# Attention followed by a feed-forward layer: the first feed-forward tile prepared inside the last attention pairs

## The reference

```
xn  = layernorm(x)                                  # eps 1e-5
q   = xn @ q_w.T + q_b
xd  = depthwise conv of xn over tokens, width 3, stride 2   # 1024 keys
k,v = xd @ k_w.T + k_b,  xd @ v_w.T + v_b
att = softmax(q k^T / 8)  v        # 16 heads of 64
A   = att @ out_w.T + out_b
e   = argmax(xn @ W_router)        # one of 4 experts per token
h   = gelu(xn @ W1[e] + b1[e])     # 1024 -> 4096
F   = layernorm(h @ Wo + bo + xn)  # 4096 -> 1024, eps 1e-12, gamma, beta
out = x + A + F
```

## Time and profile before

| | |
|---|---|
| median of 3 runs | 1966.93 us |
| lowest, highest | 1964.63, 2223.03 us |
| the profiled execution's own time | 1971.07 us |
| its span, slowest core (core 3) | 1969.5 us |
| spans of the eight cores | 1947.0 to 1969.5 us |
| busy on core 3: TensorE, VectorE, ScalarE, GpSimd | 93%, 47%, 45%, 15% |

### The profile page before, as it was taken

How to read it: one execution, slowest core, us unless ns; L and a number is a source line. 1 busy time by engine, 2 the same in 40 slices (tenths; PEclk the granted TensorE clock), 3 DMA queues, 4 the chain that set the end, 5 groups by cost and what they waited for, 6 DMA issues and landing times.

```text
span 1969.5 us, 37041 instructions; the slowest of 8 cores (1947.0 to 1969.5 us)
## 1 busy us (share of the span) xinstructions
PE 1828.8 (93%) x12540; PEld 1004.3 (51%) x12540; DVE 934.0 (47%) x1257; ACT 895.2 (45%) x1381; POOL 298.3 (15%) x357
## 2 busy tenths in 40 slices
PE   3588999998999999887899999999999999999995
PEld 1245222232554222222566666766666676666663
DVE  3354689856563888774132233413333323332225
ACT  2244988887455977775122222322222322222221
POOL 3122001001230110011001111101111111101111
PEclk9799999999999999998999999999999999999998
DMA  7759989984686999954756566856555776556551
GB/s 172 182 150 122 181 159 172 162 156 144 183 174 138 141 167 169 166 184 156 260 195 216 203 213 215 266 207 218 211 204 186 249 263 212 183 188 208 203 197 72
DMA packets 89171, 366.69 MB, mean 186 GB/s; under 512 B 11792, under 2 KB 11936, under 8 KB 68000
## 3 DMA queue, kind: packets, MB, share of 16 engines
q1 hardware_dynamic: 50112, 252.06, 38.8%
q0 software_dynamic: 38880, 112.27, 29.7%
HBM read 363.27 MB, written 94.90 MB: 233 GB/s over the span
## 4 chain that ended last, share of the span: by engine, by line
PE 73%; DMA 10%; DVE 6%; ACT 6%; issue 3%; POOL 0%; SPq 0%; DVEq 0%; ACTq 0%; POOLq 0%
PE ff_py L981 25%; PE ff_pu L946 25%; ACT pbuf L556 5%; DMA xa_d<-stg 4%; PE ps_a L505 4%; PE ps_s L543 4%; PE ps_a L569 4%; PE ps_q L367 3%; DMA row<-x 3%; DVE rc L581 3%; PE ps_q L395 2%; PE ps_m L574 2%; PE ps_q L381 2%; DMA xn_d<-row 2%; DMA stg<-x 1%
## 5 line engine op out<-in xcount | busy, mean ns | idle before, releaser
L960 ACT ACTIVATE ff_it<-ff_pu,b1t 128x256 bf16<-128x256 f32 (+1 forms) x608 | 244.3, 453 | 729.6 <-PE ff_pu L946 729.6
L556 ACT ACTIVATE pbuf<-ps_s 128x1024 bf16<-128x1024 f32 x512 | 477.3, 1061 | 116.8 <-PE ps_s L543 99.4
L946 PE MATMUL ff_pu<-ff_xg,ff_w 128*128 128x256 bf16 (+1 forms) x4864 | 516.4, 265 | 1.1 <-DVE ff_xg L930 1.1
L981 PE MATMUL ff_py<-ff_wo,ff_it 128*128 128x512 bf16 x2240 | 510.7, 381 | 3.8 <-DVE stg L511 3.8
L946 PEld LDWEIGHTS ff_pu<-ff_xg,ff_w 128*128 128x128 bf16 x4864 | 444.9, 98 | 73.4 <-issue 1.3
L981 PEld LDWEIGHTS ff_py<-ff_wo,ff_it 128*128 128x128 bf16 x2240 | 218.7, 98 | 238.2 <-issue 8.1
L581 DVE RECIPROCAL rc<-ps_m 128x512 f32<-128x512 f32 x64 | 214.7, 3355 | 44.9 <-PE ps_m L574 44.2
L569 PE MATMUL ps_a<-pbuf,v_sb 128*64 128x512 bf16 x1024 | 209.1, 404 | 5.8 <-DVE masks_all L464 4.8
L543 PE MATMUL ps_s<-qT,kT 64*128 64x512 bf16 x1024 | 201.3, 384 | 11.9 <-ACT pbuf L556 9.7
L574 PE MATMUL ps_m<-pbuf,ones 128*64 128x512 bf16 x1024 | 197.7, 381 | 0.0
L930 DVE COPY ff_xg<-ff_pt 128x1024 bf16<-128x1024 bf16 x35 | 24.2, 691 | 348.0 <-PE ff_pt L923 348.0
(11 more groups left out here) (135 smaller groups left out, 1238.7 us busy)
## 6 DMA issues: line engine op xcount, KB each, us to landing
ff_w<-scrW SPq DMA_DIRECT2D x152, 1024.0 KB
scrW<-w POOLq DMA_DIRECT2D x64, 512.0 KB, 15.6
row<-x SPq DMA_DIRECT2D x32, 512.0 KB, 6.6
xn_d<-row SPq DMA_DIRECT2D x32, 512.0 KB, 5.8
row<-xn_d SPq DMA_DIRECT2D x32, 512.0 KB, 15.8
stg<-x SPq DMA_DIRECT2D x32, 512.0 KB, 12.1
xa_d<-stg SPq DMA_DIRECT2D x32, 512.0 KB, 8.9
scrWo<-wo POOLq DMA_DIRECT2D x16, 512.0 KB, 13.0
```

The costliest lines, as they stand in the source:

```text
L556: e_at[g] = op("scalar", lambda s: s.activation(pbuf[g % 4][:, :], ps_s[g % 2][:, :], AF.Exp, scale=0.125), w)
L946: E.emit("tensor", lambda t, r_=r, q_=q, ic_=ic, c=cc, j_=j, sl=k % NW1SLOT: t.matmul(pu[r_][:, q_, 0:n], w1[:, sl, c * 512 + ic_ * 128:c ...
L960: E.emit("scalar", lambda s, r_=r, q_=q, ic_=ic, i_=i, j_=j, k_=k: s.activation(it[:, k_ % 3, ic_, 0:n], pu[r_][:, q_, 0:n], AF.Gelu, bias ...
L981: E.emit("tensor", lambda t, a_=a, o=oh, ic_=ic, i_=i, k_=k: t.matmul(py[:, 2 * a_ + o, :], it[:, k_ % 3, ic_, a_ * 128:(a_ + 1) * 128], w ...
```

## The change

Three things. The first tile's halves are cast in chunk 3 and transposed in chunk 6 of the last two pairs, half 0 in the pair before the last, half 1 in the last, into the PSUM bank `K.at` that the pair leaves free (7, then 5) instead of bank 3. The last two token tiles of the output projection get row buffers of their own, laid over `otp[0]`, whose x rows are asked for right behind the attention, when the last unit that reads `otp[0]` is done; the gather of the third feed-forward tile, in the same memory, is moved behind the tail's units and waits for the stores of these two buffers. The last five Wo pieces are asked for behind the first three up steps, one, two and two, instead of all in one place of the program, from which GpSimd's queue issued them as soon as the attention's last matmuls were done; those from the fifth on also wait for all matmuls emitted before, that is for the up step.

```diff
--- before.py
+++ after.py
@@ -155,8 +155,8 @@
     sWQ, sWK, sWV, sWO, sWR, sVB = [mksem(n) for n in ("sWQ", "sWK", "sWV", "sWO", "sWR", "sVB")]
     sX = [mksem(f"sX{i}") for i in range(4)]
     sXN = [mksem(f"sXN{i}") for i in range(4)]
-    sSTL = [mksem(f"sSTL{i}") for i in range(3)]
-    sSTS = [mksem(f"sSTS{i}") for i in range(3)]
+    sSTL = [mksem(f"sSTL{i}") for i in range(5)]
+    sSTS = [mksem(f"sSTS{i}") for i in range(5)]
     sW1 = [mksem(f"sW1_{i}") for i in range(6)]
     sWo = [mksem(f"sWo{i}") for i in range(NIS)]
     sB1 = [mksem(f"sB1_{i}") for i in range(2)]
@@ -236,7 +236,8 @@
     xd = [place(f"xd{i}", [128, CC, 256], BF16, O_OTP + i * 4 * KB) for i in range(2)]
     otp = [place(f"otp{i}", [128, HP, 512], BF16, O_OTP + i * 8 * KB) for i in range(2)]
     rc = place("rc", [128, 512], F32, O_RC)
-    stg = [place(f"stg{i}", [128, D], F32, O_STG + i * 4 * KB) for i in range(3)]
+    stg = [place(f"stg{i}", [128, D], F32, o) for i, o in enumerate(
+        [O_STG + 4 * KB * k for k in range(3)] + [O_OTP, O_OTP + 4 * KB])]
 
     ps_s = [bank(f"ps_s{i}", [128, 1024], F32, 2 * i) for i in range(2)]
     ps_q = [bank(f"ps_q{i}", [128, 512], F32, i) for i in range(4)]
@@ -487,13 +488,17 @@
             src.rearrange("b p c -> p b c")), sem, [(sT, sT.n)])
 
     stn = [0]
-    stg_free = [[], [], []]
+    stg_free = [[] for _ in range(5)]
     out_x = {}
     otp_at, op_last = {}, {}
 
     def load_out_x(gt):
-        s_ = stn[0] % 3
-        stn[0] += 1
+        if gt >= nb * NT - 2:
+            s_ = 3 + gt % 2
+            stg_free[s_] = [op_last[(nb - 1, NQB - 2)]]
+        else:
+            s_ = stn[0] % 3
+            stn[0] += 1
         out_x[gt] = (s_, dma("sync", lambda s: s.dma_start(stg[s_][:, :], x_d[gt * 128:(gt + 1) * 128, :]),
                              sSTL[s_], stg_free[s_]))
 
@@ -523,7 +528,7 @@
         for b, gt, s_, m in K.store:
             stg_free[s_] = [dma("sync", lambda s, g_=gt, s_=s_: s.dma_start(
                 xa_d[g_ * 128:(g_ + 1) * 128, :], stg[s_][:, :]), sSTS[s_], [m])]
-            if gt + 3 < (b + 1) * NT:
+            if gt + 3 < (b + 1) * NT - (2 if b == nb - 1 else 0):
                 K.xload.append(gt + 3)
         K.store = []
 
@@ -825,7 +830,7 @@
     M = {}
 
     def ffn_rows():
-        free = [t for f in stg_free for t in f]
+        free = [t for f in stg_free[:3] for t in f]
         for dst, i in ((gam, 0), (bet, 1), (bo, 3)):
             M["rows"] = dma("sync", lambda s, d_=dst, i_=i: s.dma_start(d_[:, :], row_bc(i_)), sROW, free)
         M["rows"] = dma("sync", lambda s: s.dma_start(xa[:, 0, :], row_bc(2)), sROW, [pv_last[nb - 1]])
@@ -897,7 +902,7 @@
         for a in halves(j):
             w = since(xr_free, j, a, 3) if j >= 3 else [K.perm, K.pads] + [(q, q.n) for q in sXN]
             if j == 2:
-                w.append(op_last[(nb - 1, NQB - 2)])
+                w = w + stg_free[3] + stg_free[4]
             E.emit("gpsimd", lambda g, j_=j, a_=a: g.indirect_dma_start(
                 xr[j_ % 3][:, a_, :], None, xn_d[:, :],
                 bass.IndirectOffsetOnAxis(col(j_, a_), 0)),
@@ -917,20 +922,21 @@
         c_done[(j, a)] = op("scalar", lambda s: s.copy(xb[:, a, :], xr[j % 3][:, a, :]),
                             [xr_ld[j]] + (since(t_done, j, a, 1) if j else [K.router]))
 
-    def transpose_x(j, a):
-        w = [c_done[(j, a)]] + K.bank[3]
+    def transpose_x(j, a, at=3):
+        pt = ptr if at == 3 else ps_t[at]
+        w = [c_done[(j, a)]] + K.bank[at]
         for cc in range(CC):
             E.emit("tensor", lambda t, j_=j, a_=a, c=cc: t.transpose(
-                ptr[:, c, :], xb[:, a_, c * 128:(c + 1) * 128], eye_bf[:, :]),
+                pt[:, c, :], xb[:, a_, c * 128:(c + 1) * 128], eye_bf[:, :]),
                 waits=w if cc == 0 else [], incs=[(sT, 1)] if cc == CC - 1 else [])
         t_done[(j, a)] = (sT, sT.n)
         w = [t_done[(j, a)]]
         if j >= 2:
             w.append(u_done[(j - 2, NIS - 1)])
         E.emit("vector", lambda v, j_=j, a_=a: v.tensor_copy(
-            xg[:, j_ % 2, :, a_ * 128:(a_ + 1) * 128], ptr[:, :, :]), waits=w, incs=[(sV, 1)])
+            xg[:, j_ % 2, :, a_ * 128:(a_ + 1) * 128], pt[:, :, :]), waits=w, incs=[(sV, 1)])
         tev[(j, a)] = (sV, sV.n)
-        K.bank[3] = [tev[(j, a)]]
+        K.bank[at] = [tev[(j, a)]]
 
     def up(j, i):
         k = j * NIS + i
@@ -1039,21 +1045,20 @@
     def load_wo(i):
         w = s_last[(nb - 1, min(i, NQB - 1))] if i < 6 else pv_last[nb - 1]
         wo_ld[i] = dma("gpsimd", lambda g: g.dma_start(wo[:, i, :], scrWo[i * 128:(i + 1) * 128, :]), sWo[i],
-                       [w, (sCASTO, sCASTO.n)])
+                       [w, (sCASTO, sCASTO.n), (sT, sT.n if i > 3 else 0)])
 
     def ffn(tail):
-        for a in range(2):
-            transpose_x(0, a)
         for j in range(NJ):
             for i in range(NIS):
                 up(j, i)
                 if j == 0 and i < 3:
+                    for i_ in ((3,), (4, 5), (6, 7))[i]:
+                        load_wo(i_)
                     for fn in tail[3 * i:3 * i + 3]:
                         fn()
                     if i == 2:
+                        gather_x(2)
                         ffn_rows()
-                        for i_ in range(3, NIS):
-                            load_wo(i_)
                         for j_ in range(2):
                             gather_a(0, j_)
                 if i == 0 and j >= 1:
@@ -1196,14 +1201,17 @@
         elif kc in (1, 5) and M["texp"] < NW1SLOT:
             load_w1(M["texp"])
             M["texp"] += 1
-        if P == NPAIR - 1 and kc in (3, 5):
-            cast_x(0, (kc - 3) // 2)
+        if P >= NPAIR - 2 and kc == 3:
+            cast_x(0, P - NPAIR + 2)
+        elif P >= NPAIR - 2 and kc == 6:
+            transpose_x(0, P - NPAIR + 2, K.at)
 
     attention(1, side1)
     while M["texp"] < NW1SLOT:
         load_w1(M["texp"])
         M["texp"] += 1
-    gather_x(2)
+    for gt in range(nb * NT - 2, nb * NT):
+        load_out_x(gt)
     ffn(out_tail(1))
 
     E.emit("sync", None, waits=[(sYO[0], sYO[0].n), (sYO[1], sYO[1].n)])
```

## The result

The changed kernel took 1951.8 us, the median of four runs (1950.04 to 1954.05). Its ratio to the kernel before is 0.993, 95% interval 0.9906 to 0.9953: 0.7% less, by less than 2% but clear of the spread. In absolute terms 0.7% of 1966 is 14 us. The plain medians differ by 31.3 us, because four runs of the kernel before now have a median of 1983.11 (1964.63, 1966.93, 1999.29, 2223.03). In two of these the cores of a die ran slower for a reason outside the kernel, and the ratio leaves such runs out. The comparison on another occasion gave 1955.14 us (12 runs) and a ratio of 0.9952 (0.9921 to 0.9983), that is 9 us. The two intervals have the gains from 9 to 15.5 us in common.

The account below looks back on a forecast made before the run. TensorE bounds the feed-forward part, so time saved at the seam ahead moves the end. Core 3 gains 5.8 + 8.5 = 14.3 us, core 0 11.1; 13 us taken, giving 1954 us, range 1946 to 1964.

Parts of the forecast that it names:

- new waits: At the seam: 1.1 us before the first projection unit, and 0.1 us of the first up step for transposed copies.
- The late operation: Ahead of the first projection unit: the multiplication by the last reciprocal, ending at 932.54, leaves a wait of 1.1 us.
- The pause of 0.91 us: In the attention's pair before the last: the cast moved there holds back an exponential, and TensorE pauses about 0.9 us.
- The chosen 13 us: Whole kernel: gain taken between core 3's 14.3 us and core 0's 11.1 us, giving 1954 us.
- Sum 8.5: Seam, own row buffers: waits of 1.64 and 3.79 us, 2.8 of slow clock and 0.3 of rest vanish.
- Sum for part one: 5.8: Seam and last pairs, first tile prepared earlier: 8.8 us removed, less 1.1, 0.9, 0.1 and 0.9 us of costs.
- Cost 0; gain 0: Output-weight pieces spread behind up steps: no late reader, and no gain beyond that counted for the own row buffers.
- The chance of 0.96: Whole kernel: probability that the measured time stays within 2% (39 us) of the kernel before.
- (a): Seam: DMA becomes the bound, 37 us of transfers in 35; 2 us come back, 1956 us; chance 0.06.
- (b): Attention's last pairs: cast and transposes make pauses that lower the clock; gain only 7.4, 1959.5 us; chance 0.12.
- (c): Seam's tail: early row-buffer loads come late, additions still wait, 8.5 us stay; gain 4.5, 1962.4 us; chance 0.05.
- (d): First tile's down steps: late output-weight pieces make the kernel slower, each us beyond 36 costing one; chance 0.03.

Follow-up runs that it names:

- part one alone: Kernel before with only the first tile's casts in chunk 3 and transposes in chunk 6 of the last two pairs; profiled execution 1962.64 us, no ratio.
- part three alone: Kernel before with only the output-weight pieces asked for behind the first three up steps; profiled execution 1967.63 us, no ratio.
- the late pieces: Changed kernel with the last four output-weight pieces asked for behind the fifth up step instead of the second and third; 1961.19 us in one run.

## Why the prediction was right, and where it was not

**The steps at the seam held, most to a tenth.** Predicted for core 3: seam 31.2 of work and 1.1 + 0.1 of new waits, 32.4; measured 32.47. Behind the new wait I expected no slow clock, and there was none. The late operation was the last multiplication, as named. The pause of 0.91 us in the pair before the last came in that length. The transposes cost 0.55 us each where I counted 0.44, so the pairs together grew by 2.0 instead of 1.8. (The 966.76 us that I called the end of a copy is the end of an addition into a row buffer; the 0.14 us behind it are as I read them.) For core 3 of before that makes 48.47 - 32.47 - 2.0 = 14.0 us, forecast 14.3; for core 0, 45.20 - 32.47 - 2.1 = 10.6, forecast 11.1. The chosen 13 us stand beside 14 us by the ratio and 9 by its repetition; 1954 us beside 1951.8 and 1955.1.

**The parts did not divide as I wrote them.** "Sum 8.5" for part two holds by itself: a core with core 3's seam would gain 48.5 - 40.3 = 8.2 us, and the mean core, whose waits were shorter, 4.1. "Sum for part one: 5.8" holds only with part two in place (5.8 on the mean core); alone the part brings 0.7. The sum left out what the waits on the row buffers do when TensorE comes earlier. They hang on the chain store, load, store, load in SyncE's queue. Before, its first store is asked for 12.9 to 14.0 us behind the attention's end and its last load 29.7 to 33.4; with part one alone 4.5 us behind on all cores, and 28.1 to 30.5. So 8.4 to 9.5 us at the head of the chain become 2.5 us at its last load on the mean core, because the first store, now issued right behind the burst, takes 13.6 to 17.1 us instead of 9.6 to 12.4. In part three alone, where there is no burst, it takes 6.6 to 7.8. Whether part one would keep its 5.8 us with part three and without part two was not tried.

**Part three: right, in part by luck.** "Cost 0; gain 0" holds in the changed kernel, which has no reader of these DMAs near; that it has none is the work of part two, and the prediction doesn't say so. By itself the part shows no gain, because it carries the contention from a store to a load that is read sooner.

**The size against the measured times.** In plain medians the kernel gained 31.3 us where the prediction has 13. The step that failed is the last of the sum, "The median of the runs, 1966.93, is 4.1 us below the profiled time, so its slowest core may have waited less": it takes three runs and one profile for where the slowest core stands, and keeps that fixed. The runs showed that it is not. Of the 31.3 us, 16.2 are the base: with a fourth run of 1999.29 us the median of before went from 1966.93 to 1983.11. The other 15.1 stand beside the 13. The profiled executions differ by 21.0 us. 14.0 of them are the change on core 3; the other 7.0 are the arrival: core 3 ended its attention at 928.13 us, core 5 after the change at 923.14, 5.0 us earlier although its last two pairs are 2.0 us longer. That is spread between executions, and a forecast from one profile can't hold it. That 13 us lie near the 14 of the ratio is luck in part too: the sum was made on the two cores of before that it read, with seams of 48.5 and 45.2 us, and the mean core gained 9.9. And "About 2% is what a measurement of this kernel can tell from no change" was too coarse: the interval of the ratio is some 0.24% to either side, so that this gain of 0.7% is told from none. The chance of 0.96 for within 2% was met.

**The rivals.** (a), DMA as the bound: its condition came true, the engines were at 0.93 to 0.99 for 40 us, and its price did not: TensorE waited for none of these transfers. What SyncE had asked for was slowed by what GpSimd had issued, 10.78 against 3.46 us in part three alone. By that, the trace agrees with the Trainium skill ("DMA: Bandwidth & Descriptors", "Issuing engines are not separate DMA queues"), where all issuers share the 16 engines. (b) did not come: pauses of 0.91 us and no slow clock. (c) did not come: no wait on a row buffer. (d) did not come in the changed kernel; its mechanism, brought about by the late pieces, costs what it said for each us of wait.

## What to carry to other kernels

Where an engine waits several times in a short stretch, ask of each wait what it hangs on: the engine's own progress, or a chain of transfers whose landing is set by what else is in flight. Most of the time gained ahead of the second kind can be waited away (here part one is worth 7.8 us at the seam with part two in place and 2.8 without it), and the parts of such a change must be priced together. When transfers are moved, look for the next reader in the new place: full DMA queues cost nothing while everybody has lead, and a 0.5 MB load that was read at once took three times as long here. And work slipped into a stage that two engines share evenly belongs where the one already idles for the other: the same cast cost 0.9 us in chunk 3 and nothing in chunk 5.

## What was not expected of the hardware

The landing of one load form (0.5 MB, HBM to a row buffer) took 3.46 us on core 0 before and 10.78 in part three alone, an edit that changes only when the output-weight pieces are in flight; that of a store, on core 0, took 6.87 us in part three alone and 16.34 in part one alone. The DMA engines could be kept at 0.93 to 0.99 for 40 us while TensorE never waited, at a granted clock of 1.00. What stays open is why cores reach the seam 8 to 16 us apart in one execution, and 26 in another; it decides for the most part which core is the slowest and can be larger than the whole gain, and nothing here tests it.
